# The last stage of a three-block decoder kernel: the first accumulator's rows arrive by an adding DMA on top of the second's

## What is computed

```python
x = layernorm(x + attention(x))            # linear attention, 16 heads, gated and normed
x = layernorm(x + expert_by_token_id(x))   # one of 4 experts, chosen by the token's id
x = layernorm(x + moe(x))                  # below
```

```python
probs = softmax(masked(x @ gate_weight.T)); w, e = top_k(probs, 8); w = w / sum(w)
xb[e, pos] = x[tok]
g, u = split(einsum('ech,eoh->eco', xb, gate_up_proj))
out  = einsum('eci,ehi->ech', silu(g) * u, down_proj)
final[tok] += out[e, pos] * w
```

## Time and profile before

| What | Value |
|---|---|
| time, median of 3 runs | 939.17 us |
| fastest and slowest run | 937.63, 940.34 us |
| profiled execution, its own time | 929.28 us |
| its span | 927.5 us |
| TensorE, VectorE, ScalarE, GpSimd busy | 832.2, 632.4, 400.2, 467.5 us |
| q1 (SyncE) | 99.35 MB, 31.8% of the DMA engines' span |
| q0 (GpSimd) | 55.42 MB, 24.8% |

### The profile page before, as it was taken

How to read it: one execution, slowest core, us unless ns; L and a number is a source line. 1 busy time by engine, 2 the same in 40 slices (tenths; PEclk the granted TensorE clock), 3 DMA queues, 4 the chain that set the end, 5 groups by cost and what they waited for, 6 DMA issues and landing times. The chain is left out here.

```text
span 927.5 us, 18558 instructions
## 1 busy us (share of the span) xinstructions
PE 832.2 (90%) x5958; PEld 706.5 (76%) x5959; DVE 632.4 (68%) x1441; ACT 400.2 (43%) x820; POOL 467.5 (50%) x443
## 2 busy tenths in 40 slices
PE   6899999999999889999998789999999999999700
PEld 4677777777777678888887578998998889899600
DVE  6757765577656656777777787676776776776425
ACT  4332232332332422332332046756666666666504
POOL 0242243333343321555554457767777677766354
PEclk9999999999999999999999999999999999999955
DMA  9551112111121026223222879999999999997775
GB/s 330 174 204 47 48 46 71 64 45 45 50 86 35 24 65 220 100 84 107 108 85 76 279 209 273 290 286 285 277 296 288 280 282 290 288 224 175 165 187 209
DMA packets 72573, 155.34 MB, mean 167 GB/s; under 512 B 9952, under 2 KB 10384, under 8 KB 72144
## 3 DMA queue, kind: packets, MB, share of 16 engines
q1 hardware_dynamic: 49952, 99.35, 31.8%
q0 software_dynamic: 22576, 55.42, 24.8%
HBM read 110.22 MB, written 44.52 MB: 167 GB/s over the span
## 5 line engine op out<-in xcount | busy, mean ns | idle before, releaser
L1901 POOL DMA_INDIRECT y_rows<-arena,place_token x96 | 155.2, 1616 | 77.4 <-issue 50.4
L1890 POOL DMA_INDIRECT xg<-x_rows,place_token x96 | 93.9, 978 | 38.7 <-issue 28.3
L956 PE MATMUL ps<-arena,raw 128*128 128x192 f32 x576 | 97.9, 327 | 1.6 <-DVE arena L1679 1.6
L956 PEld LDWEIGHTS ps<-arena,raw 128*128 128x128 f32 x576 | 93.8, 190 | 3.4 <-issue 2.1
L593 PE MATMUL ps<-w_hi,x_hi 128*128 128x512 f32 (+1 forms) x332 | 77.5, 355 | 10.7 <-ACT arena L993 4.7
L1763 POOL TENSOR_TENSOR arena<-arena,attn_pack 128x512 f32<-128x512 f32 x12 | 16.4, 1366 | 117.8 <-DVE arena L1311 117.8
L593 PE MATMUL ps<-w_hi,x_lo 128*128 128x512 f32 (+1 forms) x332 | 74.5, 346 | 0.0
L956 PE MATMUL ps<-arena,mid_flat 128*128 128x192 f32 x432 | 73.1, 326 | 0.0
L593 PE MATMUL ps<-w_lo,x_hi 128*128 128x512 f32 (+1 forms) x332 | 73.0, 342 | 0.0
L956 PEld LDWEIGHTS ps<-arena,mid_flat 128*128 128x128 f32 x432 | 71.1, 190 | 2.0
L593 PEld LDWEIGHTS ps<-w_hi,x_hi 128*128 128x128 f32 x332 | 52.4, 189 | 23.0 <-issue 9.3
(11 more groups left out here) (231 smaller groups left out, 1967.0 us busy)
## 6 DMA issues: line engine op xcount, KB each, us to landing
raw<-in_gu SPq DMA_DIRECT2D x24, 768.0 KB
mid_flat<-in_gu SPq DMA_DIRECT2D x18, 768.0 KB
raw<-in_dn SPq DMA_DIRECT2D x24, 256.0 KB
y_rows<-zero SPq DMA_DIRECT2D x20, 256.0 KB
mid_flat<-in_dn SPq DMA_DIRECT2D x18, 256.0 KB
arena<-in_gu SPq DMA_DIRECT2D x6, 768.0 KB
arena<-in_xT SPq DMA_DIRECT2D x16, 256.0 KB
x_res<-in_x SPq DMA_DIRECT2D x16, 256.0 KB, 2.7
```

What stands on the lines that cost most here:

```text
L956: m = pe.matmul(out, wgu[slot][:, q, part * P:(part + 1) * P], xgT[:, p, q, :], start=(q == 0), stop=(q == KC - 1))
L1890: pool.indirect_dma_start(out=xg[:, place, h, :], out_offset=None, in_=x2_d, in_offset=bass.IndirectOffsetOnAxis(ap=place_token[:, 2 * n + ...
L1901: pool.indirect_dma_start(out=y2_d if p and n < DUAL else y_d, out_offset=bass.IndirectOffsetOnAxis(ap=place_token[:, 2 * n + h:2 * n + h ...
```

## The change

The arrays of the first accumulator in SBUF, `y_all`, and the loads into it are gone. Instead GpSimd issues, on its own queue, transfers of `y_d`'s rows that add to `y2_all` in SBUF. There is no sum left on VectorE or GpSimd, and statistics, scaling and stores work on `y2_all`. Three adding transfers are issued ahead; transfer q+3 is issued behind the power of piece q. GpSimd's first one waits for all eight loads of the second accumulator and for all scatters. The loads of the second accumulator now go one at a time, with a single semaphore.

```diff
-        y_all = take("y_all", [P, NT, D])
...
-        r3_too = sem("r3_too"); r3_made = sem("r3_made"); y2_in = sem2("y2_in")
+        y2_in = sem("y2_in")
...
             for q in range(NT // 2):
-                at_least(sp, y2_in[q % 2], 16 * (q // 2))
-                sp.dma_start(y2_all[:, 2 * q:2 * (q + 1), :], y2_d[2 * q * P:2 * (q + 1) * P, :].rearrange("(j p) n -> p j n", p=P)).then_inc(y2_in[q % 2], 16)
-
-            sp.wait_ge(place_made, NG + 2)
-            for p in range(2):
-                sp.wait_ge(y_added[p], 32 * (E2 // 2))
-            for q in range(LAST):
-                at_least(sp, y_in[q % 3], 16 * (q // 3))
-                sp.dma_start(y_all[:, slice(*PIECES[q]), :], rows_of(y_d, q)).then_inc(y_in[q % 3], 16)
+                at_least(sp, y2_in, 16 * q)
+                sp.dma_start(y2_all[:, 2 * q:2 * (q + 1), :], y2_d[2 * q * P:2 * (q + 1) * P, :].rearrange("(j p) n -> p j n", p=P)).then_inc(y2_in, 16)
...
-                sp.dma_start(rows_of(d["out"], q), y_all[:, slice(*PIECES[q]), :]).then_inc(out_kept, 16)
+                sp.dma_start(rows_of(d["out"], q), y2_all[:, slice(*PIECES[q]), :]).then_inc(out_kept, 16)
...
-                    m = act.activation(y_all[:, j, :], y_all[:, j, :], ACT.Identity, bias=shift3[:, j:j + 1], scale=rstd3[:, j:j + 1])
+                    m = act.activation(y2_all[:, j, :], y2_all[:, j, :], ACT.Identity, bias=shift3[:, j:j + 1], scale=rstd3[:, j:j + 1])
...
                 dve.wait_ge(y_in[q % 3], 16 * (q // 3 + 1))
-                dve.wait_ge(y2_in[0], 4 * NT)
-                dve.wait_ge(y2_in[1], 4 * NT)
                 lo, hi = PIECES[q]
-                dve.tensor_tensor(y_all[:, lo, :], y_all[:, lo, :], y2_all[:, lo, :], ALU.add).then_inc(r3_made, 1)
-                dve.wait_ge(r3_made, q + 1)
-                if hi - lo == 2:
-                    dve.wait_ge(r3_too, q + 1)
                 for j in range(lo, hi):
-                    m = dve.bn_stats(stat3[:, j, :], y_all[:, j, :])
+                    m = dve.bn_stats(stat3[:, j, :], y2_all[:, j, :])
...
-            def last_sum(q):
...
-            last_sum(0)
+            def add_rows(q):
+
+                at_least(pool, y_in[q % 3], 16 * (q // 3))
+                pool.dma_start(y2_all[:, slice(*PIECES[q]), :], rows_of(y_d, q), accum_op=ALU.add).then_inc(y_in[q % 3], 16)
+
+            pool.wait_ge(y2_in, 8 * NT)
+            for p in range(2):
+                pool.wait_ge(y_added[p], 32 * (E2 // 2))
+            for q in range(3):
+                add_rows(q)
             for q, (lo, hi) in enumerate(PIECES):
-                if q + 1 < LAST and PIECES[q + 1][1] - PIECES[q + 1][0] == 2:
-                    last_sum(q + 1)
                 pool.wait_ge(ve_made, NT + SLOT_T + q + 1)
                 settle(pool)
                 pool.tensor_tensor(rstd3[:, lo:hi], ve3[:, lo:hi], minus_half[:, 0:hi - lo], ALU.pow).then_inc(rstd_made, 1)
+                if q + 3 < LAST:
+                    add_rows(q + 3)
```

More of the change, by code:

```diff
@@ L468, in weights_of, with rows_of @@
             return weights_in[slot], (16 if slot < 6 else 0) + 48 * (turn + 1)
+        def rows_of(rows_d, q):
+            lo, hi = PIECES[q]
+            return rows_d[lo * P:hi * P, :].rearrange("(j p) n -> p j n", p=P)
         block = ctx.enter_context(nc.Block())
@@ L565, in _ @@
             for q in range(NT // 2):
-                at_least(sp, y2_in[q % 2], 16 * (q // 2))
-                sp.dma_start(y2_all[:, 2 * q:2 * (q + 1), :], y2_d[2 * q * P:2 * (q + 1) * P, :].rearrange("(j p) n -> p j n", p=P)).then_inc(y2_in[q % 2], 16)
-            def rows_of(rows_d, q):
-                lo, hi = PIECES[q]
-                return rows_d[lo * P:hi * P, :].rearrange("(j p) n -> p j n", p=P)
-            sp.wait_ge(place_made, NG + 2)
-            for p in range(2):
-                sp.wait_ge(y_added[p], 32 * (E2 // 2))
-            for q in range(LAST):
-                at_least(sp, y_in[q % 3], 16 * (q // 3))
-                sp.dma_start(y_all[:, slice(*PIECES[q]), :], rows_of(y_d, q)).then_inc(y_in[q % 3], 16)
+                at_least(sp, y2_in, 16 * q)
+                sp.dma_start(y2_all[:, 2 * q:2 * (q + 1), :], y2_d[2 * q * P:2 * (q + 1) * P, :].rearrange("(j p) n -> p j n", p=P)).then_inc(y2_in, 16)
             for q in range(LAST):
                 sp.wait_ge(out_made, q + 1)
-                sp.dma_start(rows_of(d["out"], q), y_all[:, slice(*PIECES[q]), :]).then_inc(out_kept, 16)
+                sp.dma_start(rows_of(d["out"], q), y2_all[:, slice(*PIECES[q]), :]).then_inc(out_kept, 16)
             sp.wait_ge(out_kept, 16 * LAST)
```

## The result

| | before | changed |
|---|---|---|
| median time, 19 runs each | 937.76 us | 943.49 us |
| ratio, 95% interval | | 1.0056, 1.0041 to 1.0071 |
| span of the profiled execution | 927.5 us | 943.1 us |
| busy, VectorE and GpSimd | 632.4, 467.5 us | 625.8, 469.2 us |
| last scatter's issue to the end of the span | 39.2 us | 43.6 us |

The change makes the kernel slower by 0.56%, 5.3 us (the medians differ by 5.7). The forecast had 13.7 us. Its range, 941 to 965 us, holds the measured 943.49, but the forecast loss is more than twice the measured one. The two spans differ by 15.6 us, but that is mostly scatter between executions: the changed kernel profiled again gave 928.9 us. What repeats is the tail, and so it is read from a point that both programs have, the issue of the last scatter.

A forecast was written before the change was run, and what follows sets the result against it. The bound moves from VectorE to the DMA engines. From 892.6, adding 2.0, 0.4, 27.7, 8.5, 0.7 and 9.3 gives 941.2, 13.7 us later; on the median 952.9 us, range 941 to 965.

The forecast's parts named there:

- the rate of adding: Adding transfers in the tail: 6.6 us per MB, 27.7 us for 4.19 MB; bounds 2.7 and 7.9 us per MB.
- the price of the stores: Stores in the tail's DMA engines: six pairs stored before the last add lands, 8.5 us more.
- the exit: From the last bn_stats to the end of the span: 9.3 us, kept as before.
- start of the first adding bytes: Tail's start: first adding transfer at 892.6, when SyncE's first load started; issue 2.0 us, bytes 0.4 us behind its end.
- They don't hide each other, they add up: Plain and adding transfers, 865 to 871 us: took 5.2 us together, 5.0 if apart, so stores add their time.
- The issue: GpSimd's time to issue an adding pair: 2.0 us, bounds 1.0 and 3.8; as the bound, 955.2 us, chance 0.12.
- Three in flight: Transfer q+3 issued behind piece q's power: late by 1.4 + 2.0 us, but two others queued, so engines don't run dry.
- the cover: Two other adding transfers, 7 us of moving, queued ahead of a late-issued one; gone if adding were cheap.
- The one-in-flight loads: Second accumulator's eight loads: 4.5 us each, last at 884, no cost; at 6.4 us each 6.3 us late, chance 0.04.
- the announced signs: Profile after: issues 1.4 to 3.8 us, bn_stats 3.5 to 5 us apart, 5.4 to 7.9 us per MB, last bn_stats near 932.
- the low rate: Low end for adding transfers, 5.4 us per MB instead of 6.6: 947.8 us.
- the stores' hiding: Stores that hide fully beside the adding transfers take off 8.5 us: 944.4 us.

The follow-up runs named there:

- the staged kernel: Kernel before with adding transfers only for the last four of nine pieces, issued one at a time behind the powers of pieces 0, 1, 2 and 4; ratio 0.9975.

## Why the prediction was wrong

Its direction and its mechanism were right: the bound moved from VectorE to the DMA engines, since adding moves at about half the plain rate, and the stores run beside it. Its size was not: two terms of the sum, the rate of adding and the price of the stores, were too high, and a third, the exit, was taken to be constant. The sum, term by term, against the profiles:

| term | forecast | measured |
|---|---|---|
| start of the first adding bytes, behind the last scatter's issue | 4.3 + 2.4 us | 7.7 us (4.2 wait, 1.5 to the first issue, 2.0 to its bytes) |
| moving 4.19 MB by adding | 27.7 us, 6.6 us per MB | 23.8 us elapsed with the stores held back, 5.7 us per MB |
| stores between | 8.5 us | 4.4 us |
| behind the last bn_stats | 9.3 us | 6.9 us |
| tail against before | +13.7 us | +4.4 us |

**The rate** was mis-sized by 3.9 us. The step that took the middle between the scatters' 7.9 and the 5.4 of their faster slices gave the short scatters too much weight; at 256 rows a transfer the adding rate is close to its low bound, whatever the destination (6.0 in DRAM). The rule of the Trainium skill's page "Collectives: The Full Stack", section "The bandwidth ceiling: the fold count and why AG ≠ RS ≠ AR", two reads and half the rate, gave 5.4 and was nearer than my choice, and the measured rate came no lower than 5.7. The fit of the Trainium skill's page "DMA: Bandwidth & Descriptors", section "Anatomy of one DMA — SWDGE (gpsimd) path", gives 3.2 us for a pair. It came near for the quickest plain pair (3.6 us to landing), and not for adding ones (5.5 at least in the changed kernel).

**The stores** were mis-sized by 4.1 us. "They don't hide each other, they add up" rested on one window of 6 us with 0.20 MB of scatters in it. Holding the stores back showed 4.4 us for 2.56 MB. I also counted six pairs, 3.15 MB, where 2.56 MB were stored in time, since a pair's store is issued 6.5 us and more behind its bn_stats (the first at 917.42, for 910.94) and not some 5 behind its landing; that alone is 1.6 of the 4.1 us.

**The exit** was taken over as a constant, 9.3 us. It contained a DRAIN of GpSimd, the last releaser of the whole program, and that differed with the transfers GpSimd had issued. 2.4 us came back there; the prediction never asked what ends the 6 us behind the last activation.

**The issue**, 2.0 us, was 1.2 (1.3 for the first, and 2.2 at most where three follow one another), well inside the bounds, and GpSimd was never the bound. The 1.5 us between wait and first issue are missing in the sum. **Three in flight** kept the engines full, as argued, and the run without the add fits the other half: with cheap transfers the cover is gone. **The one-in-flight loads** took 4.4 us each for a forecast of 4.5, and landed 14 us before they were needed; they cost nothing that the runs can tell. Of the announced signs in the profile the pace (3.5 to 5 us) held only from the fifth piece on.

That the range held the result is partly luck. It took the low rate (947.8) and the stores' hiding (944.4) as separate ends, and both came at once; only the room left below them, down to 941, took in 943.49. With both, 13.7 - 3.9 - 4.1 leaves 5.7 us, with the exit 3.3, and with the late first issue, 1.0, the 4.4 of the profiles but for 0.1.

## What to carry to other kernels

An adding DMA wasn't a free sum here: it moved its bytes at about half the rate of a plain one, so it paid only where the DMA engines stood idle while an engine's sums were part of the bound, for as many bytes as that slack held, here two tiles of sixteen (0.9946) or six (0.9958), which the intervals don't tell apart, and not all sixteen (1.0056). The engine that issues it pays too, and what stands behind the issue moves: here a sum pushed by an issue came to lie beside VectorE's small instructions, and in the staged kernel the three of them lost 3.7 us. And read what ends the program behind the last real instruction: an exit's wait can be worth as much as the change.

## What the runs showed that was not expected

- GpSimd's DRAIN at the exit takes 7.70 us in the kernel before and 4.76 to 5.41 us in those with large direct transfers, 81 ns more for each late transfer, and was the last to end in both kernels compared here.
- A VectorE TENSOR_SCALAR of 128 x 2 took up to 1.93 us instead of 0.17 beside a GpSimd sum of 128 x 512.
- Adding 256 rows a transfer moved at 5.7 to 6.0 us per MB into SBUF and 6.0 in DRAM, plain ones at 2.7; scatters of 96 rows at 7.9.
